# Layer 1 of a four-layer gated attention program: loads from the sync engine, another order of work in a batch, and a full-row maximum matmul in layer 0

## What is computed

```python
xn = (x - mu) * jax.lax.rsqrt(var + EPS) * ln_g + ln_b
q = _split_heads(xn @ Wq)                      # 16 heads of 64
kv = xn @ Wkv
k = _split_heads(kv[..., :INNER]); v = _split_heads(kv[..., INNER:])
mem = _split_heads(memories @ Wm)              # memories: 6404 rows
k = jnp.concatenate([k, mem], axis=2); v = jnp.concatenate([v, mem], axis=2)
dots = jnp.einsum('bhid,bhjd->bhij', q, k) * scale
attn = jax.nn.softmax(dots, axis=-1)
out = jnp.einsum('bhij,bhjd->bhid', attn, v)   # then heads joined, @ Wo + bo
x = x + tanh(g_xattn[1]) * out
```

## Time and profile before

| | us |
|---|---|
| median of three runs | 5979.7 (5976.93 to 5980.03) |
| the profiled execution, whole time | 5979.15 |
| its span, first to last instruction | 5977.4 |
| layer 0 attention, to its last matmuls | about 0 to 330 |
| layer 1 attention, loads to last unit | about 363 to 3156 |
| PE busy over the span | 5196.6 (87%) |
| DVE / ACT / POOL busy over the span | 4557.3 / 3034.3 / 1443.0 |

### The profile page before, as it was taken

How to read it: one execution, slowest core, us unless ns; L and a number is a source line. 1 busy time by engine, 2 the same in 40 slices (tenths; PEclk the granted TensorE clock), 3 DMA queues, 4 the chain that set the end, 5 groups by cost and what they waited for, 6 DMA issues and landing times. The chain is left out here.

```text
span 5977.4 us, 75371 instructions
## 1 busy us (share of the span) xinstructions
PE 5196.6 (87%) x27320; PEld 1979.9 (33%) x27320; DVE 4557.3 (76%) x5110; ACT 3034.3 (51%) x5833; POOL 1443.0 (24%) x1136
## 2 busy tenths in 40 slices
PE   8936999999999999999992389999998589999997
PEld 4413444444444444444441122222222312222222
DVE  6346867787777767787767789999994589999993
ACT  2212444444444444444440048888885158888884
POOL 0013545454454545454450200000000200000000
PEclk9968999999999999999995679999997689999996
DMA  0023324232233324232200211111110221111100
GB/s 28 1 90 89 86 68 112 53 108 47 83 78 85 88 65 115 53 105 50 50 22 4 80 29 25 20 20 25 20 21 4 79 33 20 21 24 20 25 16 5
DMA packets 164055, 293.81 MB, mean 49 GB/s; under 512 B 26492, under 2 KB 103752, under 8 KB 160616
## 3 DMA queue, kind: packets, MB, share of 16 engines
q1 hardware_dynamic: 111560, 163.29, 10.3%
q10 hardware_dynamic: 52128, 125.71, 9.5%
HBM read 178.92 MB, written 109.89 MB: 48 GB/s over the span
## 5 line engine op out<-in xcount | busy, mean ns | idle before, releaser
L1587 DVE TENSOR_REDUCE a_mx<-ps 128x1 f32<-128x1024 f32 x1536 | 1820.1, 1220 | 151.6 <-PE ps L1467 129.3
L1554 ACT ACTIVATE a_prob<-ps 128x512 f32<-128x512 f32 (+1 forms) x3264 | 1705.3, 601 | 427.0 <-PE ps L1455 422.3
L1152 POOL TENSOR_TENSOR tot_p<-tot_p,prob 128x512 f32<-128x512 f32 (+1 forms) x896 | 1265.1, 1412 | 834.3 <-ACT prob L1040 767.6
L1074 DVE TENSOR_REDUCE mx<-ps 128x1 f32<-128x1024 f32 x896 | 1052.5, 1216 | 427.3 <-PE ps L860 427.3
L1040 ACT ACTIVATE prob<-ps 128x512 f32<-128x512 f32 (+1 forms) x1888 | 980.0, 606 | 671.3 <-PE ps L885 570.9
L1467 PE MATMUL ps<-a_K,a_Q 51*128 51x512 bf16 (+1 forms) x3328 | 1068.4, 385 | 49.8 <-DMA a_Q<-q_stack_dram 30.4
L1455 PE MATMUL ps<-a_Q,a_K 51*128 51x512 bf16 (+1 forms) x3264 | 1003.7, 389 | 82.8 <-ACT a_prob L1554 76.7
L1491 PE MATMUL ps<-a_prob,a_V 128*9 128x512 f32 x6528 | 953.9, 609 | 10.9 <-ACT a_acc L1538 10.9
L896 PE MATMUL ps<-prob,V 128*64 128x512 f32 (+1 forms) x3776 | 954.8, 615 | 0.0
L884 PE MATMUL ps<-QA,KA 128*128 128x512 f32 (+1 forms) x1888 | 854.7, 453 | 73.5 <-ACT prob L1040 72.7
L1097 DVE TENSOR_TENSOR tot_d<-tot_d,prob 128x512 f32<-128x512 f32 x928 | 831.2, 896 | 75.7 <-ACT prob L1040 24.5
(11 more groups left out here) (348 smaller groups left out, 3348.6 us busy)
## 6 DMA issues: line engine op xcount, KB each, us to landing
a_K<-k_stack_dram SPq DMA_DIRECT2D x64, 600.4 KB, 5.9
k_hi_dram<-hi_s SPq DMA_DIRECT2D x112, 256.0 KB, 2.0
k_lo_dram<-lo_s SPq DMA_DIRECT2D x112, 256.0 KB, 2.1
KA<-k_hi_dram ACTq DMA_DIRECT2D x64, 384.0 KB, 4.3
KA<-k_lo_dram ACTq DMA_DIRECT2D x64, 384.0 KB, 5.5
KB<-k_hi_dram ACTq DMA_DIRECT2D x64, 384.0 KB, 6.5
k_bf_dram<-bf_s SPq DMA_DIRECT2D x112, 128.0 KB, 2.6
KM<-k_bf_dram ACTq DMA_DIRECT2D x32, 448.0 KB, 6.6
```

What stands on the lines that cost most here:

```text
L1074: nc.vector.tensor_reduce(mx[:, u % 2, j, i % FULL:i % FULL + 1], c.banks(slot(n), 2), AX.X, ALU.max).then_inc(released, 1)
L1152: nc.gpsimd.tensor_tensor(tot_p[0:r, u % 2, :], tot_p[0:r, u % 2, :], p, ALU.add).then_inc(totalled_p, 1)
L1554: nc.scalar.activation(prob[0:r, batch % 2, t % BATCH, :], c.banks(n % 3)[0:r, :], ACT.Exp, scale=SCALE).then_inc(exped, 1)
L1587: nc.vector.tensor_reduce(mx[:, u % 2, j, i % FULL:i % FULL + 1], c.banks(slot(step), 2), AX.X, ALU.max).then_inc(maxed, 1)
```

## The change

In **layer 1**:

- All loads of keys and queries are issued by SP (with waits on the score and maximum matmuls that they must follow), between its stores; ACT issues none in the main phase.
- PE's batch becomes: two maxima steps, four score tiles, the extra (and `turn_nm`), then `weigh` of the batch before. DVE: maxima, then the sums of the same batch, then the extra; POOL sums the same batch too. ACT copies the accumulator (`take_acc`) after the extra.
- `turn_nm` is one matmul with a 4-row result in place of four with 1-row results; `take_nm` is four small activations in place of one copy.
- POOL adds `tot_d` to `tot_p` at a unit's end, and `finish` drops its four matmuls over `tot_d`.
- Before unit 0 the 15 `project_v` stand between the 17 `project`, and all maxima come after them (before, maxima were interleaved with V tiles from the sixth on).
- The phase that cleared tiles is merged with the load phase ahead of `norm`, which now loads the first weights too; `c.y` is cleared in the main phase.

In **layer 0**: `ones` and `nmT` have 128 partitions (zeros beyond the fourth), and x and the weights are issued by SP ahead of the memory.

```diff
-        ones4 = sb("ones4", [UQ, P], FP32R)
+        ones = sb("ones0", [P, P], FP32R)
...
-        nmT = sb("nmT", [UQ, N], FP32R)
+        nmT = sb("nmT", [P, N], FP32R)
...
+                    sp.dma_start(c.x[:], x_in.rearrange("(t p) d -> p t d", p=P)).then_inc(x_in_done, 16)
+                    for i, name in enumerate(("Wk", "Wv", "Wq", "Wo")):
+                        sp.dma_start(W[:, i, :], w[name]).then_inc(weights_in, 16)
...
-                    act.dma_start(c.x[:], x_in.rearrange("(t p) d -> p t d", p=P)).then_inc(x_in_done, 16)
-                    for i, name in enumerate(("Wk", "Wv", "Wq", "Wo")):
-                        act.dma_start(W[:, i, :], w[name]).then_inc(weights_in, 16)
...
-                    nc.vector.memset(f32(ones4[:]), 1.0)
+                    nc.vector.memset(f32(ones[:]), 1.0)
+                    nc.vector.memset(f32(nmT[:]), 0.0)
...
-                    nc.tensor.matmul(out, ones4[:, 0:r], nmT[:, cols], start=False, stop=True).then_inc(scored, 1)
+                    nc.tensor.matmul(out, ones[:, 0:r], nmT[:, cols], start=False, stop=True).then_inc(scored, 1)
...
-    HEAD_START = 5
     for k in range(JOBS):
         takes_slot("k", k)
-    for g in range(BATCHES):
-        takes_slot("v", (0, g))
-        if g >= HEAD_START:
-            for n in range(2 * (g - HEAD_START), 2 * (g - HEAD_START) + 2):
-                takes_slot("max", divmod(n, STEPS))
...
+    POOL_SUMS = POOL_TILES + 1
...
-        load(c, [(gain[:], w["ln_g"].partition_broadcast(P)), (shift[:], w["ln_b"].partition_broadcast(P)),
-                 (bo[:], w["bo"].partition_broadcast(P))], "l1")
-        norm(c, gain, shift)
-
-        with phase(nc, "chain", "cleared") as (block, chain, cleared):
+        with phase(nc, "loaded") as (block, loaded):
+            @block.sync
+            def _(sp):
+                sp.dma_start(gain[:], w["ln_g"].partition_broadcast(P)).then_inc(loaded, 16)
+                sp.dma_start(shift[:], w["ln_b"].partition_broadcast(P)).then_inc(loaded, 16)
+                sp.dma_start(bo[:], w["bo"].partition_broadcast(P)).then_inc(loaded, 16)
+                for base in (0, DH):
+                    sp.dma_start(Wo_twice[0][base:base + DH, :], w["Wo"][0:DH, :]).then_inc(loaded, 16)
+                sp.wait_ge(loaded, 16 * 9)
+
+            @block.scalar
+            def _(act):
+                act.dma_start(weights[0][:, W_Q, :], w["Wq"][:, 0:P]).then_inc(loaded, 16)
+                act.dma_start(weights[0][:, W_K, :], w["Wkv"][:, 0:P]).then_inc(loaded, 16)
+                act.dma_start(weights[0][:, W_V, :], w["Wkv"][:, HEADS * DH:HEADS * DH + P]).then_inc(loaded, 16)
+                act.dma_start(weights[0][:, W_M, :], w["Wm"][:, 0:P]).then_inc(loaded, 16)
...
-                nc.vector.memset(c.y[:], 0.0)
...
+        norm(c, gain, shift)
...
-                load_weights(0)
-                load_wo(0)
+                def load_max(h):
...
+                    if h >= 2:
+                        sp.wait_ge(slotted, slot_no["max", (2 * h - 3, STEPS - 1)] + 1)
...
+                def load_q(u):
...
+                    if u >= 2:
+                        sp.wait_ge(scored, ring_no(u - 2, TILES - 1) + 1)
...
+                def load_segment(h, s):
...
+                    if h >= 1:
+                        sp.wait_ge(scored, ring_no(2 * h - 1, min((s + 1) * SEG, TILES) - 1) + 1)
...
                 for k in range(JOBS):
                     store(k)
-                for p in range(PAIRS):
-                    load_wo(2 * p + 1)
-                    if p + 1 < PAIRS:
-                        load_weights(p + 1)
-                        for k in range((p + 1) * JOBS, (p + 2) * JOBS):
-                            store(k)
-                        load_wo(2 * p + 2)
+                load_max(0)
+                load_q(0)
+                for s in range(SEGS):
+                    load_segment(0, s)
+                load_q(1)
+                load_max(1)
+                for u in range(UNITS):
+                    if u % 4 == 0:
+                        load_wo(u // HALVES + 1)
+                        if u // 4 + 1 < PAIRS:
+                            load_weights(u // 4 + 1)
+                    if u % 4 == 2 and u + 2 < UNITS:
+                        load_wo(u // HALVES + 1)
+                    for b in range(BATCHES):
+                        kind, what = extra_of(u, b) or (None, None)
+                        if kind == "k":
+                            store(what)
+                        for t in tiles_of(b):
+                            if u % HALVES == 1 and u + 1 < UNITS and (t % SEG == SEG - 1 or t == TILES - 1):
+                                load_segment(u // HALVES + 1, t // SEG)
+                    if u + 2 < UNITS:
+                        load_q(u + 2)
+                    if u % HALVES == 1 and (u + 3) // 2 < HEADS:
+                        load_max((u + 3) // 2)
...
-                    for j in range(UQ):
-                        last = nc.tensor.matmul(c.banks(n % 3)[0:1, j * P:(j + 1) * P], nm[:, u % 2, j:j + 1],
-                                                c.ident[:], start=True, stop=True)
-                    last.then_inc(scored, 1)
+                    nc.tensor.matmul(c.banks(n % 3)[0:UQ, 0:P], nm[:, u % 2, :], c.ident[:], start=True, stop=True
+                                     ).then_inc(scored, 1)
...
-                    pe.wait_ge(totalled_d, DVE_TILES * (u + 1))
-                    pe.wait_ge(totalled_p, POOL_TILES * (u + 1))
+                    pe.wait_ge(totalled_p, POOL_SUMS * (u + 1))
                     for j in range(UQ):
                         cols = slice(j * P, (j + 1) * P)
                         nc.tensor.matmul(c.banks(bank)[:, cols], acc[:, u % 2, cols], Wo_twice[h % 2][:],
                                          start=True, stop=True)
-                        nc.tensor.matmul(c.banks(bank + 1)[:, j:j + 1], tot_d[:, u % 2, cols], ones_col[:],
-                                         start=True, stop=False)
                         last = nc.tensor.matmul(c.banks(bank + 1)[:, j:j + 1], tot_p[:, u % 2, cols], ones_col[:],
-                                                start=False, stop=True)
+                                                start=True, stop=True)
                     last.then_inc(slotted, 1)
...
                 for k in range(JOBS):
                     project(k)
-                for g in range(BATCHES):
-                    project_v(0, g)
-                    if g >= HEAD_START:
-                        for n in range(2 * (g - HEAD_START), 2 * (g - HEAD_START) + 2):
-                            max_score(*divmod(n, STEPS))
-                for n in range(2 * (BATCHES - HEAD_START), STEPS + LEAD):
+                    if k < BATCHES:
+                        project_v(0, k)
+                for n in range(STEPS + LEAD):
                     max_score(*divmod(n, STEPS))
                 turn_nm(0)
                 for u in range(UNITS):
                     for b in range(BATCHES):
+                        for step in max_steps(u, b):
+                            max_score(*step)
                         for t in tiles_of(b):
                             score(u, t)
-                        for step in max_steps(u, b):
-                            max_score(*step)
-                        if b >= 1:
-                            weigh(u, b - 1)
-                        elif u >= 1:
-                            weigh(u - 1, BATCHES - 1)
                         kind, what = extra_of(u, b) or (None, None)
                         if kind == "k":
                             project(what)
                             finish(what)
                         if b == NM_AT and u + 1 < UNITS:
                             turn_nm(u + 1)
+                        if b >= 1:
+                            weigh(u, b - 1)
+                        elif u >= 1:
...
+                    for j in range(UQ):
+                        last = nc.scalar.activation(QB[u % 2][DH:DH + UQ, j * P:(j + 1) * P], c.banks(n % 3)[0:UQ, 0:P],
+                                                    ACT.Copy, scale=c.ident[0:UQ, j:j + 1])
+                    last.then_inc(exped, 1)
...
-                load_max(0)
-                load_q(0)
-                load_q(1)
-                for s in range(SEGS):
-                    load_segment(0, s)
-                load_max(1)
-                for g in range(BATCHES):
-                    take_v(0, g)
+                    if k < BATCHES:
+                        take_v(0, k)
                 take_nm(0)
...
-                            if u % HALVES == 1 and u + 1 < UNITS and (t % SEG == SEG - 1 or t == TILES - 1):
-                                load_segment(u // HALVES + 1, t // SEG)
-                        if b == 0 and u >= 1:
-                            take_acc(u - 1)
                         kind, what = extra_of(u, b) or (None, None)
...
-                    if u + 2 < UNITS:
```

(22 more changed lines are left out.)

70 lines of the change are left out of this document (34 added, 36 removed).

## The result

The changed kernel takes 5707.9 us (median of four runs, 5706.18 to 5709.09); the kernel before, beside it, 5979.6. The ratio is 0.9546 with a 95% interval of 0.953 to 0.9563: 272 us, or 4.5%, faster. The profiled execution spans 5705.1 us.

A forecast was written before the change was run, and what follows sets the result against it. In layer 1's attention PE was taken to set the pace, so only what it executes or waits for counts. The terms summed to -242 from 5979.15 us: 5737, stated as 5740, range 5680 to 5840.

The forecast's parts named there:

- loads off ACT: At 14 starts of a head in layer 1, PE's gap and the slow clock go when SP issues the loads: -122.
- projections, and lag of DVE and POOL: Layer 1's batches: most of PE's wait before projections goes, -25; units' ends, POOL's further sums and DVE's lag cost +20.
- turn_nm: Layer 1's units: a quarter of the 33.9 us of PE for 256 instructions stays: -24.
- finish: Layer 1's units: 256 matmuls go, 35.9 us busy but overlapping: -26, between -18 and -36.
- start of layer 1: Ahead of unit 0: clearing phase and wait for weights go, first score at 491 instead of 522.47: -31.
- layer 0 tiles: Layer 0: longer steps into and out of the maximum matmul go, 0.10 + 0.19 us over 100 tiles: -29.
- layer 0 start: Layer 0's beginning: x, first in SP's queue, lands earlier, but memory and small vectors late: -5.
- Rivals 1 and 5: Heads' starts: SP's late loads keep wait and slow clock, 5800 to 5862; or ACT's issues aren't the cause, 5862; together 0.08.
- the walk: One layer 1 batch with a projection, followed step by step: PE waits about 0.25 us for cut_lo in place of 0.55.
- VectorE and GpSimd: Layer 1's units: units' ends, POOL's further sums, and lag met by a projection or finish: +20, bounds 0 to +60.
- The second and third rival: DVE slightly the bound, 5815 to 5855 (0.13); both sums of a batch wait for POOL's, slower than before, 6175 (0.05).
- Rival 4: Layer 1's batches: the new order hides all of the projections' wait and nothing lags: 5690; chance 0.12.

The follow-up runs named there:

- e2: The changed kernel with the old order of a batch back on PE, ACT, DVE and POOL; 5734.7 us.
- e10: The changed kernel with turn_nm again as four matmuls with 1-row results and one copy on ACT; 5726.0 us.
- e6: The changed kernel with ones and nmT of layer 0 over 4 partitions again; 5747.4 us.
- e7: The changed kernel with ones and nmT of layer 0 over 64 partitions; 5742.6 us.
- e1: The changed kernel with the main loop's loads of keys and queries issued by ACT again; 5807.3 us.
- e12: The changed kernel with POOL adding one column of each tile in place of 512, its sums left out of the result; 5656.0 us.
- e4: The changed kernel, but in the batch with finish DVE sums one tile and POOL three, in place of two and two; 5668.7 us.
- e11: The changed kernel with one more DVE operation in each of the 480 batches, a 128x128 copy that nobody waits for; 5866.7 us.
- e9: The kernel of e4, but finish with both groups of sum matmuls again and no addition of tot_d on POOL; 5700.7 us.
- e5: The changed kernel, but finish with both groups of sum matmuls again and no addition of tot_d on POOL; 5712.1 us.

## Why the prediction held, term by term

| term | forecast | measured | from |
|---|---|---|---|
| loads off ACT | -122 | -120 | units before to e2, -162.5, less the two matmul terms (a remainder) |
| projections, and lag of DVE and POOL | -25 + 20 | -27 | e2 |
| turn_nm | -24 | -20 | e10 |
| finish | -26 | -22 | plain unit 70.4 to 69.1 in e2, -1.3 x 32 = -42, less turn_nm |
| start of layer 1 | -31 | -34 | first score -80.6, less layer 0 |
| layer 0 tiles | -29 | -40 | first score to last, 233.9 to 194.4; e6. The rows alone: -35, e7 |
| layer 0 start | -5 | -7 | first score of layer 0, 80.55 to 73.42 (71.5 to 74.1 in the other runs) |
| sum | -242 | -270 | |

**Loads: right in mechanism and size**, and the largest term. The reading of unit 22 against unit 29 gave it, and e1 shows the cause: same work, the issues put back on ACT, gap and slow clock back. The trace before gives the price once more: 72 us in the 14 gaps and half of the 105 us behind them make 124. The price depends on what stands around it (96 us in the new order, about 120 in the old). Rivals 1 and 5 are out: no wait for a load stands in the units.

**Projections: the walk was right for about every second batch.** It had `cut_lo` end some 0.25 us after PE wants the projection's slot, in each batch with a projection. In unit 4 the next score stands 0.77 us behind the first maxima matmul in one batch (796.37 to 797.14) and 0.55 in the next (801.95 to 802.50), which is the distance without a wait:

```profile
795.99 0.68 DVE L1080 TENSOR_TENSOR lo_s<-ps,hi_s 128x512 fp32r<-128x512 f32 x1
796.37 0.84 PE L922 MATMUL ps<-KM,QM 64*128 64x512 bf16 x4
...
801.95 0.62 PE L922 MATMUL ps<-KM,QM 64*128 64x512 bf16 x4
```

The step that was off is the last one, from one batch to all: a batch in which PE waits is mostly followed by one in which it doesn't. Over all batches behind a projection that distance is 0.66 us on average, and 0.51 in e12, where nothing holds PE. So 0.15 us stay and not 0.25, 16 to 18 us in all (119 projections; e12 lies 16 below e4) in place of 30.

What the new order is worth without the wait behind `finish` shows between e2 and e4: 62.8 us, of which 51 lie in the units with projections and 8 in those with u % 4 = 3, whose V groups the prediction gave no term. The forecast was 25. It counted the 105 waits that the rows show for 119 projections, left too much of them, and left out the V groups.

**VectorE and GpSimd: right in mechanism, too small.** The prediction named lag met by a `finish` as part of its +20; it is the only long wait left in the units, 28.4 us by the rows and 35 by e4. It took the sums of a batch to stay near 2.36 us; beside POOL they are 2.86 there. So both halves of -25 + 20 were too small, -25 for about -63 and +20 for +35, and the errors are of opposite sign. That the two together missed by 22 us only (-5 for -27), and not by the first half's 38, is luck.

The second and third rival did not come, but e11 shows how little was missing in the batches with a projection: the copies add 10.7 us to unit 4, which has nine of them. The prices of both rivals rest on a miscount: `extra_of` leaves 225 batches without an extra and not 257 (119 have a projection, 105 a V group, 31 a `finish`); with it the third rival's 435 is 429.

**finish: right before the change of order, wrong after it.** Its matmuls are worth 22 to 30 us wherever PE doesn't wait behind them (e9, the old order). In the changed kernel they gain 5 (e5), since the wait for DVE took their place. The prediction kept the two in separate terms and did not see that one takes from the other; the table's -22 is the price in the old order. Saving PE's time ahead of a wait for another engine bought nothing in the units that have the wait.

**Layer 0: the term was mis-sized, by a step that the row group left out.** The step behind the weighing was not walked; the earlier trace rows end with it. The next score stands 0.56 us behind it where the trace after has 0.45; that third step is 0.11 us in a plain tile. In the 22 or 23 tiles that hold a maxima step the whole gain is 0.28 us (2.51 to 2.23), so the step makes some 6 of the missing 11 us. The other 4 to 5 are the slow clock of the first tiles, which nobody forecast and which no run ties to the rows. Both steps that the rows show went, so the lower bound (-10) did not come.

**Start of layer 1: the walk held to about 3 us.** From the first projection to the loads 48 us were forecast and 47.7 measured, to the first maxima 57 and 56.7, to the first score 98 and 95.8. With layer 0 taken out, the first score is 34 us earlier.

The sum of the terms missed by 28 us: layer 0's tiles are 11 of them and the batch order 22; the rest is small and of both signs. Rival 4 had all of the projections' wait go and nothing lag. Most of that wait went, but DVE's lag at `finish` came.

## What to carry to other kernels

DMA issues in the stream of an engine that others wait for cost the wait and then the clock: look at the granted clock beside each gap. When an order of work is changed, ask of each shared buffer which instruction takes it next, and who frees it; walk two rounds and not one, since a wait in the first can be slack in the second. And when DVE and GpSimd both read SBUF, count DVE's time as it is beside GpSimd, and take work off DVE in the one batch where someone waits for it.
